# Graph attention on Trainium2: a stack's block moved by one transfer, and one graph normalised in each of four slots

## The reference, cut to what matters

```python
h = jnp.maximum(_layernorm(x, axis=-1), 0.0)
q = _split_heads(h @ Wq + bq)          # k and v alike
scores = jnp.einsum('bhqd,bhkd->bhqk', q, k) / jnp.sqrt(HD)
scores = scores + beta * adj_e
scores = jnp.where(adj_e > 0, scores, -9e15)
probs = jax.nn.softmax(scores, axis=-1)
out = jnp.einsum('bhqk,bhkd->bhqd', probs, v)
x = x + out
```

## Time and profile before

| what | value |
|---|---|
| runs | 1095.65, 1099.44, 1101.88 us; median 1099.44 |
| profiled execution | 1097.34 us, its span 1095.6 us |
| granted TensorE clock over the span, mean | 0.985 |
| instructions | 33283 |
| busy: POOL | 664.4 us (61%) |
| DMA | 163.16 MB, mean 149 GB/s |
| issues of q_st and k_st | 384 and 384, 96.0 KB each |
| transposing issues | 62 |

### The profile page before, as it was taken

How to read it: one execution, slowest core, us unless ns; L and a number is a source line. 1 busy time by engine, 2 the same in 40 slices (tenths; PEclk the granted TensorE clock), 3 DMA queues, 4 the chain that set the end, 5 groups by cost and what they waited for, 6 DMA issues and landing times.

```text
span 1095.6 us, 33283 instructions
## 1 busy us (share of the span) xinstructions
PE 995.5 (91%) x10587; PEld 673.5 (61%) x10587; DVE 934.0 (85%) x4250; ACT 907.4 (83%) x2378; POOL 664.4 (61%) x908
## 2 busy tenths in 40 slices
PE   4689999999999999999999898999999999999996
PEld 2356666656666666666666566666666666666664
DVE  6469889888898888988899788798888889888898
ACT  3369788878888988888898788888888988888997
POOL 2846656557566666666566656566666656666642
PEclk9899999999999999999999999999999999999999
DMA  4465676647677656667665667656677765667641
GB/s 153 109 145 136 140 170 162 151 117 160 155 177 162 161 143 131 165 160 177 152 161 136 133 163 167 150 148 141 154 161 177 162 140 152 148 154 172 148 118 45
DMA packets 188255, 163.16 MB, mean 149 GB/s; under 512 B 112816, under 2 KB 163504, under 8 KB 188080
## 3 DMA queue, kind: packets, MB, share of 16 engines
q1 hardware_dynamic: 187552, 160.24, 61.7%
q10 hardware_dynamic: 528, 0.79, 0.2%
HBM read 35.91 MB, written 25.17 MB: 56 GB/s over the span
## 4 chain that ended last, share of the span: by engine, by line
PE 40%; issue 10%; SPq 9%; ACT 8%; DMA 4%; DVE 3%; POOL 1%; ACTq 0%; DVEq 0%; POOLq 0%
PE ps_p L442 24%; PE ps_t L462 8%; ACT probs L520 6%; SPq L250 6%; PE ps_s L454 4%; DMA hT<-h_parts 3%; SPq L264 3%; PE ps_o L477 1%; ACT pT L554 1%; DVE biased L644 1%; PE ps_o L478 1%; PE ps_o L479 1%; DVE pT L650 1%; ACT hn L535 1%; POOL on L348 1%
## 5 line engine op out<-in xcount | busy, mean ns | idle before, releaser
L520 ACT ACTIVATE probs<-biased,neg_max 128x128 f32<-128x128 f32 x1536 | 489.8, 392 | 133.5 <-DVE neg_max L644 111.7
L644 DVE CUSTOM_DVE_ANT_0 biased<-ps_s,mask 128x128 f32<-128x128 f32 x1536 | 354.7, 286 | 120.9 <-PE ps_s L454 115.8
L442 PE MATMUL ps_p<-hT,w 128*128 128x512 f16 x1728 | 426.4, 388 | 18.4 <-DMA hT<-h_parts 12.8
L348 POOL TENSOR_TENSOR on<-on,xb 128x384 f32<-128x384 f32 x128 | 127.6, 997 | 284.7 <-DVE on L665 284.7
L442 PEld LDWEIGHTS ps_p<-hT,w 128*128 128x128 f16 x1728 | 170.7, 100 | 179.8 <-issue 32.6
L650 DVE TENSOR_TENSOR pT<-ps_t,pT 128x512 f16<-128x512 f32 x384 | 263.2, 686 | 0.9 <-ACT pT L554 0.2
L462 PE MATMUL ps_t<-ident,probs 128*128 128x128 f32 x1536 | 247.0, 284 | 14.6 <-ACT probs L520 12.1
L554 ACT ACTIVATE pT<-ps_t 128x512 f16<-128x512 f32 x384 | 221.9, 578 | 0.3 <-PE ps_t L462 0.3
L442 PE MATMUL ps_p<-w,hT 128*128 128x384 f16 x1152 | 207.6, 326 | 0.0
L454 PEld LDWEIGHTS ps_s<-k_st,q_st 96*128 96x128 f16 x1536 | 116.1, 98 | 127.8 <-issue 56.1
L454 PE MATMUL ps_s<-k_st,q_st 96*128 96x128 f16 x1536 | 149.8, 219 | 42.5 <-issue 34.9
(11 more groups left out here) (65 smaller groups left out, 998.5 us busy)
## 6 DMA issues: line engine op xcount, KB each, us to landing
q_st<-qT SPq DMA_DIRECT2D x384, 96.0 KB, 2.2
k_st<-kT SPq DMA_DIRECT2D x384, 96.0 KB, 2.2
out<-on SPq DMA_DIRECT2D x128, 192.0 KB, 2.1
xs<-in_x SPq DMA_DIRECT2D x31, 768.0 KB, 5.1
adjs<-in_adj SPq DMA_DIRECT2D x32, 256.0 KB, 5.4
hT<-h_parts SPq DMA_TRANSPOSE x62, 5.7
xs<-in_x ACTq DMA_DIRECT2D x1, 768.0 KB, 7.4
k_st<-in_L_gnn_Wq SPq DMA_DIRECT2D x1, 576.0 KB, 5.2
```

Source lines behind the costliest of these rows:

```text
L348: pool.tensor_tensor(on[:, j % 2, :], on[:, j % 2, :], xb[:, par, j, :], ALU.add).then_inc(added, 1)
L442: mm = pe.matmul(dst, stationary, moving, start=m == 0, stop=m == MMS - 1)
L520: act.activation(probs[:, odd, i, :], biased[:, odd, i, :], ACT.Exp, bias=neg_max[:, odd, i:i + 1], scale=-1.0).then_inc(exp_done, 1)
L644: dve.tensor_tensor_reduce(out=biased[:, odd, i, :], in0=ps_s[:, i * N:(i + 1) * N], in1=mask[:, gp, v // CH, :], scale=-1.0, scalar=3.0e3 ...
```

## The change

It has two parts. First, each block of a stack is moved by one transfer: 128 partitions of qT or kT to 32 partitions of the stack, four places each. For that, the columns of q's and k's weights and biases are put in another order, so that in a chunk the four heads of one dimension lie on neighbouring partitions (partition 4e + i holds dimension e of head place i), and place i of chunk c is head 3i + c. v keeps its order; `values_of` picks the head accordingly. The reordering is made where the weights are split at the start, chunk by chunk, with three instructions for each weight instead of one. Second, ACT normalises one graph at the end of each of slots 3, 4, 5 and 6.

```diff
@@ heads and dimensions of a row of 384
+        def heads_first(row):
+            return row.rearrange("p (i e) -> p e i", i=HPC)
+
+        def dims_first(row):
+            return row.rearrange("p (e i) -> p e i", i=HPC)
@@ spread
-                    for i in range(HPC):
-                        sp.dma_start(dst[HD * b:HD * (b + 1), par, i],
-                                     src[HD * i:HD * (i + 1), part]).then_inc(landed, 16)
+                    sp.dma_start(dst[HD * b:HD * (b + 1), par], src[:, part]).then_inc(landed, 16)
@@ scores (and the same factor in high_part)
-                    pe.wait_ge(q_in, 16 * 3 * HPC * (g + 1))
-                    pe.wait_ge(k_in, 16 * 3 * HPC * (g + 1))
+                    pe.wait_ge(q_in, 16 * 3 * (g + 1))
+                    pe.wait_ge(k_in, 16 * 3 * (g + 1))
@@ values_of
-                    h = c * HPC + i
+                    h = i * CH + c
@@ step of ACT
-                    if ahead and u in (3, 4):
-                        for j in range(2 * (u - 3), 2 * (u - 2)):
-                            normalise(s + 1, 1 - par, j)
+                    if ahead and 3 <= u < 3 + G:
+                        normalise(s + 1, 1 - par, u - 3)
@@ weights_high
-                act.activation(w[:, 0, :, W_COLS[n]], w_raw[:, :, W_COLS[n]], ACT.Copy, scale=SHRINK).then_inc(w_high, 1)
+                for c in range(CH):
+                    out, raw = w[:, 0, c, W_COLS[n]], w_raw[:, c, W_COLS[n]]
+                    if n < 2:
+                        out, raw = dims_first(out), heads_first(raw)
+                    act.activation(out, raw, ACT.Copy, scale=SHRINK).then_inc(w_high, 1)
@@ weights_low
-                dve.wait_ge(w_high, n + 1)
-                dve.scalar_tensor_tensor(out=w[:, 1, :, W_COLS[n]], in0=w_raw[:, :, W_COLS[n]], scalar=SHRINK,
-                                         in1=w[:, 0, :, W_COLS[n]], op0=ALU.mult, op1=ALU.subtract).then_inc(w_low, 1)
+                for c in range(CH):
+                    low, raw, high = w[:, 1, c, W_COLS[n]], w_raw[:, c, W_COLS[n]], w[:, 0, c, W_COLS[n]]
+                    if n < 2:
+                        low, raw, high = dims_first(low), heads_first(raw), dims_first(high)
+                    dve.wait_ge(w_high, CH * n + c + 1)
+                    dve.scalar_tensor_tensor(out=low, in0=raw, scalar=SHRINK, in1=high, op0=ALU.mult,
+                                             op1=ALU.subtract).then_inc(w_low, 1)
```

More of the change, by code:

```diff
@@ L429, in project @@
                 if first == 0 and n == 0 and s == 0:
-                    pe.wait_ge(w_low, ("q", "k", "v").index(kind) + 1)
+                    pe.wait_ge(w_low, CH * (("q", "k", "v").index(kind) + 1))
                 for m in range(first, end):
@@ L546, in high_part @@
                 if n == 0:
-                    wait(act, q_in if kind == "q" else k_in, 16 * 3 * HPC * s)
+                    wait(act, q_in if kind == "q" else k_in, 16 * 3 * s)
                 dst, b = (qT, 0) if kind == "q" else (kT, 1)
@@ L723, in _ @@
                                      op1=ALU.mult).then_inc(wq_scaled, 1)
-            dve.scalar_tensor_tensor(out=b_scaled[:, 0, :], in0=b_row[:, 0, :], scalar=SCALE,
-                                     in1=gap[:, 0, :].bitcast(F32), op0=ALU.mult, op1=ALU.mult).then_inc(b_scaled_done, 1)
+            dve.scalar_tensor_tensor(out=dims_first(b_scaled[:, 0, :]), in0=heads_first(b_row[:, 0, :]), scalar=SCALE,
+                                     in1=heads_first(gap[:, 0, :].bitcast(F32)), op0=ALU.mult,
+                                     op1=ALU.mult).then_inc(b_scaled_done, 1)
             dve.wait_ge(qk_scaling, 9)
-            dve.tensor_tensor(b_scaled[:, 1, :], b_row[:, 1, :], gap[:, 1, :].bitcast(F32),
-                              ALU.mult).then_inc(b_scaled_done, 1)
+            dve.tensor_tensor(dims_first(b_scaled[:, 1, :]), heads_first(b_row[:, 1, :]),
+                              heads_first(gap[:, 1, :].bitcast(F32)), ALU.mult).then_inc(b_scaled_done, 1)
             def weights_low(n):
-                dve.wait_ge(w_high, n + 1)
-                dve.scalar_tensor_tensor(out=w[:, 1, :, W_COLS[n]], in0=w_raw[:, :, W_COLS[n]], scalar=SHRINK,
-                                         in1=w[:, 0, :, W_COLS[n]], op0=ALU.mult, op1=ALU.subtract).then_inc(w_low, 1)
+                for c in range(CH):
[5 more added lines that the diff above has]
+                                             op1=ALU.subtract).then_inc(w_low, 1)
             first_low_part(ps_h[0], 0)
```

## The result

The kernel after takes 1256.3 us (median of 4 runs, 1252.6 to 1261.2), the one before 1099.2: a ratio of 1.143, 95% interval 1.138 to 1.149. The prediction was 1076, in a range of 1028 to 1126, with a chance of 0.26 for slower. The miss, 180 us, is larger than the width of that range.

The account below looks back on a forecast made before the run. PE was taken as the bound, tied in a ring to SP's queue. A step of 23.1 + 8.5 + 0.2 = 31.8 us instead of 32.6 saved 25 us over 31 steps, the start cost 1.5: 1076 us, range 1028 to 1126.

Parts of the forecast that it names:

- What bounds the kernel: PE leads, 91% busy, in a ring with SP's queue: late transposes delay k, late k delays PE's scores (34.9 us).
- k_in: PE's wait for k's spread before the scores: data landed at 6.0 us against 6.5 wanted, so the 1.2 us wait goes.
- The issues: SP's transfers for q and k: 24 issues a step become 6, 0.6 us each, 1.9 us a spread instead of 8.1.
- Its data don't shrink: Data of a spread on the DMA engines: the same 1.18 MB, 5 us from the 0.64 share, bounds 2.5 and 7.5.
- The normalisations: ACT's four in slots 3 to 6: last ends 11.9 us after the scores instead of 7.4; PE regains 0.5 us.
- The sum of 23.1 us: From q projection to transposes on SP: 6.5 + 11.9 + 1.5 + 2.1 + 1.1, against 23.4 us before.
- The flight of 8.5 us: The transposing pair on SP's queue, from first issue to landing of hT: taken as 8.5 us.
- The floor of 30.1 us: PE's step without the k wait and ACT's backlog: 31.8 - 1.2 - 0.5 us.
- The slow clock: PE's clock after its new idle time at hT: 0.2 us a step added.
- (b): At q projections, late normalisation makes hT a long wait with a slow clock, 1.0 us a step: 1132 us; chance 0.17.
- (c): Spread paced by data, no faster than before; k stays 1.2 us late at the scores: 1113 us; chance 0.09.
- The start: Weights cut into 18 parts instead of 6 at the start, strided reads: 0 to 4 us, 1.5 taken.

Follow-up runs that it names:

- every third partition: Kernel after, still one transfer per block, but blocks interleaved so that block b writes partitions b, b + 3, b + 6 and so on: 1132.2 us, ratio 1.029.
- the second part alone: Kernel before with only the normalisations changed, one in each of slots 3, 4, 5 and 6: 1158.6 us, ratio 1.056.
- the best run: Kernel after with blocks interleaved at step 3 and GpSimd's two sums moved between the second and third split: 1040.3 us, ratio 0.949.
- the run with every third partition and two slots: Kernel after with blocks interleaved at step 3 and two normalisations each in slots 3 and 4, as before: 1060.0 us, ratio 0.969.

## Why the prediction was wrong, point by point

**What bounds the kernel.** Right: the 34.9 us called "issue" were k_in. They nearly went when k's data came sooner (3.7 us with every third partition) and grew when they came later (86.8).

**The issues.** Right: 0.62 us each, 1.87 a spread. SP's queue was relieved as worked out.

**"Its data don't shrink".** This is the step that failed, and it is worth most of the miss: 1256 us fall to 1132 when only the destination partitions are changed. The share of 0.64 gave 5 us for the data of a spread, with 2.5 and 7.5 as bounds. Measured: 1.18 MB at 134 GB/s is 8.8 us, and k's last block landed 11.7 us after the first issue where 6.0 was forecast. The share of 0.64 told how full the engines were with *those* transfers; it was carried to another shape as if the rate of a full engine were fixed. The row of q's spread says the same: 133 GB/s at a share of 0.56 would be 238 GB/s at a full one, 5 us again, and a full one of the new shape moved 134. The prediction even said that the destination stays on 32 partitions while the source gets 128. Its bound for no gain, 7.5 us, was the length of a window with the old transfers; no row was of the new shape.

**k_in.** Followed from it: 6.0 us after the projection was expected, against 6.5 wanted. In the step shown the scores begin 10.6 us after it (558.75 - 548.14), 4.1 late. With the step between partitions mended the 6.0 was nearly right: PE waits before the scores in six steps only, 3.7 us in all.

**The normalisations** are the second step that failed, by size. The order behind them was right. The sum of 23.1 us from the q projection to the transposes was 25.3 at the median with every third partition, where k hardly delays anything, and 26.0 instead of 24.3 in the second part alone. The step shown there, a short one, puts 1.0 us of it before the end of the last normalisation and 0.5 in GpSimd's split; steps with a slow clock at their start have 25.6 at the median, the others 25.0. Where the rest of it lies was not followed. So even with k's data in time the kernel takes 1132.2 us, outside the range. The flight of 8.5 us was right: 8.7 at the median in both runs. The floor of 30.1 us wasn't reached: the best run, at 1040 us, has a step of 30.6 us.

**The slow clock** is the third term that was mis-sized. 0.2 us a step was put in for hT's new wait, a guess that no run shows; the runs show more. The second part alone spent 21.5 us more of PE's busy time, 0.7 us a step, the kernel after 57 us, 1.8 a step, there for two waits in each step. The fall doesn't strike each time. In the kernel after, the 4.4 us behind a wait for hT had a granted clock under 0.8 in 16 of 26 cases and 1.00 in ten, in the second part alone in 14 of 28. The length of the wait alone doesn't decide it: in the second part alone one of 1.88 us was followed by 0.61 and one of 3.34 us, at 848.24, by 1.00. The 1.7 us that (b) sets for one slow stretch is 4.2 x (1 - 0.59) for the window behind the wait at 519.32; the 4.4 us at 0.61 from 548.10 on in the kernel after lose as much.

**The rivals.** (c) had the right mechanism, a spread paced by its data, and the wrong price: it stopped at "no faster than before" (1113), and its evidence against itself, the share of 0.64, was a share of another shape; the new spread does show a share of about 1, as (c) asked. For the new transfers 1.87 us of issuing stand against 8.8 us of data; for the old ones the 12 issues took 8.1 of 9.8 us. (b) is what the second part does. With k's data in time its 1132 us met 1132.2, with waits of 2.5 us for hT and a slow clock behind half of them. That the number fits so well is partly luck: (b) wanted a flight of 9.5 us, and it was the start of the transposes that was late. Neither rival allowed for the other; together they give 1256.

**The start.** 1.5 us were set for the split in 18 pieces. DVE's low parts of q and k, read with a stride in three pieces each, take 2.24 and 3.30 us, where one instruction had taken 1.34 and 1.35; v's, three pieces without a stride, take 1.50 after 2.02. The first transposed h is used at 57.19 us instead of 55.73, but in the run with every third partition and two slots, which has the same pieces, at 55.94: the pieces explain some 0.2 us of it at most.

## What to carry to other kernels

A DMA share read while a queue feeds the engines slowly says how full they are with that shape, and no more: here 0.56 at 133 GB/s, and 1.04 at 134 GB/s with the new one. Before transfers are merged, ask at what step between partitions they will write. Why the step matters is not shown here; measured is that a step of 3 between destination partitions, free of charge because a contraction doesn't care about the order of its rows, turned a loss of 13% into a gain of 3%, with all else equal, and that a step of 4 with a fourth block gained the same 3%. And before work is moved later on one engine, follow every queue that waits in order behind it to the end: moving two sums on GpSimd was worth 51 us in one loop and 92 in another.

## What the runs showed of the hardware that was not expected

The rate of transfers from 128 partitions into 32 rows, one for each block, depends on the step between the rows: 134, 129, 215 and 328 GB/s for steps of 1, 2, 3 and 4, at DMA shares of 1.04, 1.00, 0.98 and 0.90. With the same step 3, the run with two slots has 207 at 0.94. The same bytes into the same 32 neighbouring partitions, as four transfers of 32 partitions each, were issued by SP in 8.57 us and moved at 133 GB/s with a share of only 0.56; and with each of the four reading every fourth partition, at 141 GB/s with 0.38. A fourth block and a contraction over 128 partitions instead of 96 cost nothing that shows: 1059.2 us against 1060.0.
